# Order of gathers and adds in a routed feed-forward: lists laid out by tile, a third bank for y, weight pieces spread by one line

## The reference

```python
x = x + cross_attention(layernorm(x), ctx)      # 16 x 56 tokens, 1500 context rows of 512 each
h = layernorm(x)                                 # 896 tokens
scores = sigmoid(h @ gate_w.T) + bias            # 16 experts
topk_w, topk_idx = top_k(scores, 4)              # weights normalised to sum 1
out  = sum over the 4 experts e of a token:  w_e * (silu(h @ Wg[e].T) * (h @ Wu[e].T)) @ Wd[e].T
out += silu(h @ Sg.T) * (h @ Su.T) @ Sd.T        # shared expert, all tokens
x = x + out
```

## Time and profile before

| | |
|---|---|
| median of 3 runs | 545.14 us (544.95 to 545.25) |
| profiled execution, its own time | 546.24 us |
| its span | 544.5 us |
| TensorE busy | 481.4 us, 88% |
| VectorE, ScalarE, GpSimd busy | 48%, 29%, 22% |
| issue of a gather on GpSimd, shortest and median | 0.95 and 1.01 us |
| weight loads, issue to landing, median | 7.5 us |
| weight loads start at | 307.97, 315.36, 331.09, 340.44, 348.74, 359.55, 385.94, 407.38, 416.70, 438.94, 455.00 us |

### The profile page before, as it was taken

The page is one execution under the profiler, slowest core; times in us unless marked ns, Lnnn a source line. Parts: engine busy times, 40 slices in busy tenths (PEclk is TensorE's granted clock), DMA queues, the critical chain, the costliest instruction groups (busy, mean ns, idle before and its releaser), DMA issues.

```text
span 544.5 us, 10804 instructions
## 1 busy us (share of the span) xinstructions
PE 481.4 (88%) x2472; PEld 291.5 (54%) x2473; DVE 260.0 (48%) x707; ACT 155.8 (29%) x303; POOL 119.3 (22%) x100
## 2 busy tenths in 40 slices
PE   4999999999999999998789869779998898899960
PEld 1565354453636363543358636567776666676740
DVE  3223345462737354352537864625565466555420
ACT  0001321020202020210213253435455456444430
POOL 1000000000000000000002233335554465335531
PEclk9989999999999999999899979979999899899985
DMA  9999999999999999999646676785858687445452
GB/s 212 393 419 427 398 424 415 409 427 396 424 402 426 403 422 404 422 426 415 258 127 174 150 202 191 235 254 94 221 100 265 137 207 210 78 88 98 98 64 32
DMA packets 28231, 149.04 MB, mean 274 GB/s; under 512 B 4072, under 2 KB 4200, under 8 KB 16424
## 3 DMA queue, kind: packets, MB, share of 16 engines
q1 hardware_dynamic: 15832, 123.08, 57.1%
q0 software_dynamic: 8720, 20.21, 20.5%
q10 hardware_dynamic: 3664, 5.57, 3.3%
HBM read 133.84 MB, written 15.01 MB: 273 GB/s over the span
## 4 chain that ended last, share of the span: by engine, by line
PE 49%; DMA 33%; issue 7%; DVE 3%; ACT 2%; POOLq 1%; ACTq 1%; POOL 1%; DVEq 1%; SPq 0%
DMA ctx_cols<-in_ctx_t 15%; PE b L680 13%; PE scores L550 11%; PE b L574 8%; DMA taken<-h_rows,take_at 8%; DMA out<-y_sb,add_at 5%; PE b L538 4%; PE b L500 4%; PE scores L512 2%; PE scores L680 2%; PE b L564 1%; DMA w_qk<-in_wk 1%; DMA out<-y_sb,shared_at 1%; DMA h_rows<-h 1%; POOL out L459 1%
## 5 line engine op out<-in xcount | busy, mean ns | idle before, releaser
L550 PE MATMUL scores<-ctx_cols,g_t 128*64 128x500 f32 x384 | 85.2, 586 | 2.6 <-DMA ctx_cols<-in_ctx_t 2.5
L574 PE MATMUL b<-ctx_rows,probs_t 125*64 125x512 f32 (+1 forms) x384 | 86.0, 598 | 0.0
L459 POOL DMA_INDIRECT out<-y_sb,add_at x34 | 54.5, 1604 | 89.0 <-ACT add_at L931 46.8
L423 POOL TENSOR_TENSOR rstd<-var_eps,neg_half 128x1 f32<-128x1 f32 x16 | 8.8, 549 | 268.4 <-DVE var_eps L1022 268.4
L680 PE MATMUL b<-w_hi,taken_hi 128*128 x136 | 56.2, 414 | 1.1 <-ACT taken_hi L908 1.1
L680 PE MATMUL b<-w_lo,taken_hi 128*128 x136 | 54.8, 403 | 0.0
L1280 DVE TENSOR_TENSOR w_lo<-w_raw,w_hi (+1 forms) x33 | 39.7, 1223 | 30.2 <-ACT w_hi L897 26.6
L550 PEld LDWEIGHTS scores<-ctx_cols,g_t 128*64 128x64 f32 x384 | 26.1, 136 | 51.8 <-issue 46.0
L574 PEld LDWEIGHTS b<-ctx_rows,probs_t 125*64 125x64 f32 (+1 forms) x384 | 26.3, 137 | 48.0 <-issue 47.1
L444 POOL DMA_INDIRECT taken<-h_rows,take_at x34 | 42.7, 1257 | 28.4 <-DVE take_at L1306 20.2
L897 ACT CAST w_hi<-w_raw (+1 forms) x33 | 33.8, 1047 | 29.0 <-PE b L680 9.1
(11 more groups left out here) (213 smaller groups left out, 677.2 us busy)
## 6 DMA issues: line engine op xcount, KB each, us to landing
ctx_rows<-in_ctx SPq DMA_DIRECT2D x48, 1024.0 KB, 19.5
ctx_cols<-in_ctx_t SPq DMA_DIRECT2D x32, 1500.0 KB, 22.8
w_raw<-in_experts SPq DMA_DIRECT2D x11, 1536.0 KB, 7.5
h_rows<-h ACTq DMA_DIRECT2D x16, 115.5 KB
taken<-h_rows SPq DMA_DIRECT2D x7, 264.0 KB, 3.1
out<-xs ACTq DMA_DIRECT2D x2, 784.0 KB
shared_raw<-in_shared SPq DMA_DIRECT2D x1, 1536.0 KB, 32.4
xs<-in_x ACTq DMA_DIRECT2D x12, 112.0 KB
```

What stands on the lines that cost most here:

```text
L459: nc.gpsimd.indirect_dma_start(out[:, :], bass.IndirectOffsetOnAxis(ap=add_at[i][:, 0:1], axis=0), y_sb[:, i * DIM:(i + 1) * DIM], None, c ...
L550: last = nc.tensor.matmul(scores[HALF * b:HALF * (b + 1), n, 0:CHUNK], g_t[:, k, HALF * b:HALF * (b + 1)], ctx_cols[:, at:at + CHUNK], sta ...
L574: last = nc.tensor.matmul(b3[HALF * b:HALF * (b + 1), :], probs_t[0:rows_in(p), at:at + HALF], ctx_rows[0:rows_in(p), g, b, c * DIM:(c + 1 ...
```

## The change

- **Lists in tile order.** `place_at` holds the 112 columns in float32. TensorE transposes it, ScalarE keeps the transposed copy (`place_t`), and one more matmul with a 0/1 matrix (`tile_picks`) gives 52 columns in the order of the tiles. `tile_rows` makes `tile_at` and `tile_to` from them, so tile t's column is column t-7, without a table. `T_COL` and `T_EXPERT` go; the expert of each tile is a row of `expert_row`, with which `take_weight` now picks the token's weight by comparison over 16 columns. `name_take` waits for these steps.
- **Orders.** VectorE does `take_weight(t+1)` and `name_take(t+3)` before `silu_rows(t)`. A gather waits in addition for the transposes of the tile whose buffer it fills.
- **Three y banks.** y of the expert tiles goes to PSUM banks `(t+1) % 3` of `scores`; ScalarE keeps y(t-3) in the step of tile t. `y_sb` still has two buffers.
- **Scatter columns on GpSimd.** `name_add` goes from ScalarE; `add` copies the column itself, once the add two tiles back has landed. GpSimd's loop is `gather(t+5)`, `add(t)`.
- **Weight pieces.** The count for tile t is (t-6)/34 x 33 + 4, at least what this tile needs (and the next expert's three pieces on the last tile of an expert), at most what the three slots can hold.

```diff
             def gather(t, i):
                 pool.wait_ge(take_named, t - (SHARED - 1))
                 settle(pool)
+                pool.wait_ge(tt_ready, t - 1)
+                settle(pool)
                 nc.gpsimd.indirect_dma_start(
...
             def add(t, i):
                 first = entry(pool, T_FIRST, t - SHARED, TILES + SHARED)
-                pool.wait_ge(added[0], pool.snap((first + 1) // 2 * 16 + 16, min_val=16, max_val=16 * TILES))
+                pool.wait_ge(added[i], t // 2 * 16 + 16)
                 settle(pool)
-                pool.wait_ge(added[1], pool.snap(first // 2 * 16 + 16, min_val=16, max_val=16 * TILES))
-                settle(pool)
-                pool.wait_ge(add_named, t - (SHARED - 2))
+                nc.gpsimd.tensor_copy(add_at[i][:], tile_to[:, bass.ds(t - SHARED, 1)]).then_inc(add_named, 1)
+                others = first // 2 if i == 0 else (first + 1) // 2
+                pool.wait_ge(added[1 - i], pool.snap(others * 16 + 16, min_val=16, max_val=16 * TILES))
                 settle(pool)
                 pool.wait_ge(ysb_ready, t + 1)
+                settle(pool)
+                pool.wait_ge(add_named, t + 1)
...
                     t = pair * 2 + (SHARED + k)
+                    gather(t + 5, k)
                     add(t, 1 - k)
-                    gather(t + 5, k)
...
+            def lay_places():
+                pe.wait_ge(plan_ready, 1)
+                pe.wait_ge(places_ready, 1)
+                nc.tensor.transpose(scores[:, 2, 0:P], place_at[:], ident).then_inc(places_laid, 1)
+            def pick_tiles():
+                pe.wait_ge(places_kept, 1)
+                nc.tensor.matmul(scores[:, 2, P:P + AHEAD], place_t[:], tile_picks[:], start=True, stop=True
+                                 ).then_inc(tiles_picked, 1)
...
             shared_transpose(6)
+            lay_places()
             down(4, 0, shared_hi, shared_lo, 0)
+            pick_tiles()
             up_hi(6, 0, shared_hi, shared_lo, 0)
...
-                keep_y(t - 2, i)
-                if not isinstance(t, int):
-                    name_add(t - 2, i)
+                if not isinstance(t, int) or t > SHARED:
+                    keep_y(t - 3, 1 - i)
                 more_thirds(t + 1)
...
             half(t, 0)
+            keep_y(t - 3, 1)
             keep_y(t - 2, 0)
-            name_add(t - 2, 0)
             keep_y(t - 1, 1)
-            name_add(t - 1, 1)
             z_to_hi(t)
             keep_y(t, 0)
-            name_add(t, 0)
...
+            def tile_rows():
+                dve.wait_ge(tiles_picked, 1)
+                places = scores[:, 2, P:P + AHEAD]
+                ch.mark(nc.vector.tensor_copy(tile_at[:], places))
+                ch.mark(nc.vector.tensor_scalar(wrapped[:], places, float(PAIR_TOKENS), float(TOKENS), ALU.is_lt, ALU.mult))
+                ch.link(nc.vector.tensor_scalar(empty_at[:], places, float(TOKENS), float(PAIR_TOKENS), ALU.is_ge, ALU.mult))
+                ch.link(nc.vector.tensor_tensor(wrapped[:], wrapped[:], empty_at[:], ALU.add))
+                nc.vector.scalar_tensor_tensor(tile_to[:], places, -float(PAIR_TOKENS), wrapped[:], ALU.add, ALU.add
+                                               ).then_inc(tiles_named, 1)
...
             def step(t, i):
                 z_to_lo(t - 1)
+                take_weight(t + 1, 1 - i)
+                name_take(t + 3, 1 - i)
                 silu_rows(t, i)
                 taken_to_lo(t + 1)
-                take_weight(t + 1, 1 - i)
-                name_take(t + 3, 1 - i)
                 more_thirds(t + 1)
```

More of the change, by code:

```diff
@@ L36 @@
 TILES = 48
-TABLES = 8
+TABLES = 6
 SHARED = TOKENS // P
-T_TURNS, T_COL, T_EXPERT, T_PIECES, T_TURN, T_FIRST, T_LOAD, T_HALF = (i * TILES for i in range(TABLES))
+Y_BANKS = 3
+AHEAD = TILES + 4
+T_TURNS, T_PIECES, T_TURN, T_FIRST, T_LOAD, T_HALF = (i * TILES for i in range(TABLES))
 C_ID, C_TRI, C_IOTA, C_REGION = 0, P, 2 * P, 2 * P + EXPERTS
@@ L196, in moe_attention_kernel @@
         fill = sb("fill", [P, LISTS])
[L197 to L200, removed]
+        place_at = sb("place_at", [P, LISTS + EXPERTS])
+        place_t = sb("place_t", [P, P])
+        tile_picks = sb("tile_picks", [P, AHEAD])
+        expert_row = sb("expert_row", [P, AHEAD])
+        picked_w = sb("picked_w", [P, 2 * EXPERTS])
+        wrapped = sb("wrapped", [P, AHEAD])
+        empty_at = sb("empty_at", [P, AHEAD])
+        tile_at = sb("tile_at", [P, AHEAD], i32)
+        tile_to = sb("tile_to", [P, AHEAD], i32)
         behind = sb("behind", [P, 1])
@@ L484, in _ @@
                     t = pair * 2 + (SHARED + k)
+                    gather(t + 5, k)
                     add(t, 1 - k)
-                    gather(t + 5, k)
             t = n_inner * 2 + (SHARED - 2)
-            add(t, 1)
             gather(t + 5, 0)
-            for k in range(1, 6):
+            for k in range(6):
                 add(t + k, 1 - k % 2)
@@ L613, in lay_tables @@
                 last.then_inc(table_rows_ready, 1)
+                for at, column in ((C_PICK, place_col), (C_EXPERT, expert_t)):
+                    last = nc.tensor.matmul(scores[:, 0, at:at + AHEAD], column[:].to_broadcast([P, P]),
+                                            ident[:, 0:AHEAD], start=True, stop=True)
+                last.then_inc(picks_ready, 1)
+            def lay_places():
[6 more added lines that the diff above has]
+                                 ).then_inc(tiles_picked, 1)
             pe.sem_inc(ht_ready, 1)
@@ L709, in down @@
                 settle(pe)
-                if not isinstance(t, int) or t > 1:
+                if not isinstance(t, int):
+                    pe.wait_ge(ysb_ready, t - 2)
+                    settle(pe)
+                elif t > 1:
                     pe.wait_ge(ysb_ready, t - 1)
-                    settle(pe)
+                bank = y_bank(pe, t)
                 for k in range(KI):
-                    part(y_banks[i], zt_hi, hi, at + UP, k, DIM, start=(k == 0))
-                    part(y_banks[i], zt_hi, lo, at + UP, k, DIM)
+                    part(bank, zt_hi, hi, at + UP, k, DIM, start=(k == 0))
+                    part(bank, zt_hi, lo, at + UP, k, DIM)
                 pe.wait_ge(zt_lo_ready, t + 1)
@@ L718, in down @@
                 for k in range(KI):
-                    last = part(y_banks[i], zt_lo, hi, at + UP, k, DIM, stop=(k == KI - 1))
+                    last = part(bank, zt_lo, hi, at + UP, k, DIM, stop=(k == KI - 1))
                 last.then_inc(yt_ready, 1)
@@ L925, in keep_y, with keep_places @@
                 settle(act)
-                nc.scalar.copy(y_sb[:, i * DIM:(i + 1) * DIM], y_banks[i]).then_inc(ysb_ready, 1)
-            def name_add(t, i):
-                col = entry(act, T_COL, t - SHARED, LISTS + EXPERTS - 1)
-                nc.scalar.copy(add_at[i][:], list_to[:, bass.ds(col, 1)]).then_inc(add_named, 1)
+                nc.scalar.copy(y_sb[:, i * DIM:(i + 1) * DIM], y_bank(act, t)).then_inc(ysb_ready, 1)
+            def keep_places():
+                act.wait_ge(places_laid, 1)
+                nc.scalar.copy(place_t[:], scores[:, 2, 0:P]).then_inc(places_kept, 1)
             done = act.alloc_register("act_thirds")
@@ L1154, in _ @@
             nc.vector.tensor_copy(shared_at[:], shared_place[:]).then_inc(shared_named, 1)
-            for rows in (list_at, list_to):
-                ch.mark(nc.vector.tensor_scalar(rows[:, LISTS:], dump_row[:].to_broadcast([P, EXPERTS]), -float(P), None,
-                                                ALU.add))
+            ch.mark(nc.vector.tensor_scalar(place_at[:, LISTS:], dump_row[:].to_broadcast([P, EXPERTS]), -float(P), None,
+                                            ALU.add))
             wide = [P, PAIRS, TILES_MAX]
@@ L1372, in _ @@
             list_rows()
-            dve.wait_ge(plan_ready, 1)
-            name_take(SHARED, 1)
             shared_silu(5)
             taken_to_lo(6)
+            tile_rows()
+            dve.wait_ge(dve_step, ch.now())
+            name_take(SHARED, 1)
             name_take(SHARED + 1, 0)
```

100 lines of the change are left out of this document (59 added, 41 removed).

## The result

The changed kernel takes 554.78 us (551.09 to 556.12, 4 runs) against 545.19 us (544.95 to 548.41, 4 runs) beside it: ratio 1.0155, 95% interval 1.0108 to 1.0202. It is slower; 541.2 was forecast and 548 was the top of the range. Run again it took 553.31 us, ratio 1.0142 (1.0099 to 1.0185).

The account below looks back on a forecast made before the run. The prediction took TensorE's expert-tile transposes, stalled by late gathers, plus the tail as the bound. Hand-over +1.5, start -3.5, pieces -4.7, late gathers -0.7, tail +3.5 gave -3.9 us: 541.2, own range 538.5 to 544, wider 536.5 to 548.

Parts of the forecast that it names:

- The new orders cancel: Steady loop: later y and gather ahead of add leave gathers about where they were, 4.7 instead of 4.98 us; gain 0.7 us.
- No term, but it moves which gathers they hit: Even line: weight loads start one to three tiles sooner and hit other gathers; priced at nothing.
- The third rival: The wait only moves: start gain given back, loads hit first tiles at 2.3 us each; about 545.4 us, chance 0.20.
- The sign that was named: Sign of a wrong forecast: stalls at tiles 23 to 27 of over 5 us together, from loads beside first-tile adds.
- The pieces: Tiles 30 to 32: the even line of weight pieces gains 4.7 us of 6.3 lost, bounds 2.5 and 6.3.
- The start: First expert tiles: gather(12) leaves 4.8 us sooner, add(7) 2.2 later; gain 3.5 us, bounds 1 and 5.5.
- Hand-over: Before tile 7: the new list steps make take_at(7) and its gather 1.5 us later; cost 1.5, bounds 0.5 and 3.
- Tail: After tile 40's transposes: y(37) kept only behind the last tanh, add(37) 4.2 us later; cost 3.5, bounds 2 and 4.5.
- GpSimd's copy: Scatter column copy in GpSimd's add: taken as hidden in the wait for y; bounds nothing to 0.5 us in 29 tiles.
- the slower rival: GpSimd's scatter column copy makes gathers late in most tiles: 552.9 us, or 547 at half the tiles; chance 0.20.

Follow-up runs that it names:

- 5: The changed kernel run again, nothing altered: 553.31 us, ratio 1.0142 to the kernel before.
- 7: The changed kernel with y kept one tile earlier, at t-2 as before: 541.32 us, ratio 0.9909.
- 3: The changed kernel loading only 64 of 3072 weight columns for experts past the third (stale weights): 536.93 us, ratio 0.9755.
- 4: The kernel before, loading only 64 of 3072 weight columns for experts past the third (stale weights): 536.00 us, ratio 0.9734.
- 9: The changed kernel with the scatter column copied by ScalarE instead of GpSimd: 548.32 us, ratio 1.0065.
- 1: The changed kernel with the old table of weight pieces: 552.17 us, ratio 1.0072.
- 18: The changed kernel with the old table of weight pieces, run again in a later group: 550.50 us, ratio 1.0083.
- 17: The changed kernel with the old table of weight pieces and the scatter column copied by ScalarE: 550.61 us, ratio 1.0095.
- experiment 2: The kernel before with only the new even line of weight pieces added: 548.40 us, ratio 1.0031.
- 8: The changed kernel with y kept at t-2 and zt_hi of tile 40 ahead of y of tile 39: 540.14 us, ratio 0.9906.
- 16: The changed kernel with y at t-2, tile 40's zt_hi ahead of tile 39's y, old piece table; a repeat: 537.55 us, ratio 0.9779.
- 10: The changed kernel with y at t-2, tile 40's zt_hi ahead of tile 39's y, old piece table: 536.83 us, ratio 0.9840.
- 14: The changed kernel with the scatter column copied by ScalarE and small weight loads past the third expert: 535.48 us, ratio 0.9744.
- 15: The changed kernel with y at t-2, tile 40's zt_hi first, old piece table, scatter column copied by ScalarE: 537.32 us, ratio 0.9773.

## Why the prediction was wrong

**The new orders cancel: right, but a gain was given away.** The forecast said that y one tile later and the gather ahead of the add leave each gather at the same place, 4.7 us behind the tile that frees its buffer. It leaves at 4.65 where nothing is late. But the forecast took the late y as given and never priced it: against y kept at t-2 it costs 12.0 us (5 and 7), by the two spans 4.8 of it in the tail and 6.9 between T(7) and T(40), where the gathers have less room.

**"No term, but it moves which gathers they hit": the step that failed.** The forecast gave nothing for loads that fall on other gathers and adds. Measured: +7.2 us in T(16) to T(30), +6.7 when run again, and -2.3 without the traffic (3 against 4), so it is the traffic that costs. With 1.2 us of margin, a load beside the add ahead of a first tile and the next load beside the gather behind it cost 6 us at a time, and the changed kernel has that twice. The third rival had the mechanism at 2.3 us for each, but its sum holds only 0.7 us for it, and its 545.4 is 9 us short. The sign that was named, stalls at tiles 23 to 27, did not come (tile 23 waited 1.2 us); the stalls are at tiles 17 to 19, 28 and 29.

**Is it the even line, with its sooner loads? That stays open.** T(16) to T(30) is 79.60 us before. In kernels with the late y and full loads it is, with the line, 86.77, 86.27 and, with the copy on ScalarE (9), 78.41; with the old table 84.90 (1), 80.93 (18) and 80.13 (17). In 18 a load starts at 386.44, within 0.5 us of where it was before, and tile 18 still waits 3.9 us for a gather issued at 385.25. So the same orders with any of these places of the loads give anything from no loss to 7 us. By the ratios two pairs say that the line costs 0.6 to 0.8% (1.0155 and 1.0142 with it, 1.0072 and 1.0083 without), and with y early 0.9906 stands against 0.9840 and 0.9779. The pair with the copy on ScalarE says the opposite (9 with the line 1.0065, 17 without it 1.0095), and in the kernel before experiment 2 leaves it open (0.9977 to 1.0085). No group has both tables with full loads on one set of orders, and of these pairs only 8 and 16 have intervals that do not meet. With the old table the changed kernel is still 0.7 to 0.8% slower; in the profiles of 1 and 18 T(7) is 2.4 and 1.4 us later, T(16) to T(30) 5.3 and 1.3 longer, T(32) to T(40) 0.8 and 0.7, and the tail 3.8, less what the start and the pieces gave.

**The pieces: right size, half the cause.** Forecast -4.7 for T(30) to T(32), measured -4.6 and -4.7. But the line alone gives -2.5 (2), and the changed kernel with the old table already has 12.56 (1) and 13.76 (18) for 16.59. VectorE's triple steps before and in experiment 1, each time ScalarE's three pieces, VectorE's three, and TensorE behind them:

```profile
463.20 2.95 ACT L897 CAST w_hi<-w_raw  x3 [2.16 <-PE b L680]
...
466.19 3.50 DVE L1280 TENSOR_TENSOR w_lo<-w_raw,w_hi  x3 [1.76 <-ACT w_hi L897]
...
470.16 1.19 PE L680 MATMUL scores<-w_hi,zt_lo 128*128 x2 [2.02 <-DVE zt_lo L1315]
```
```profile
467.44 2.95 ACT L948 CAST w_hi<-w_raw  x3 [1.05 <-PE scores L725]
...
468.82 3.56 DVE L1337 TENSOR_TENSOR w_lo<-w_raw,w_hi  x3 [1.59 <-ACT w_hi L948]
...
472.87 0.70 PE L725 MATMUL scores<-w_hi,zt_lo 128*128 x2 [0.32 <-DVE zt_lo L1375]
```

VectorE starts 2.99 us behind ScalarE before, and 1.38 in experiment 1: the same three pieces end early enough. With y early and full loads the line did not help there at all (15.08 us in kernel 8, against 13.96 and 13.84 with the old table in 10 and 16). Which of the new orders moved VectorE was not tried.

**The start: half of it.** Forecast -3.5, measured -1.8. The step was right: gather(12) leaves at 345.75 and not 348.47, tile 12's wait of 5.21 us is gone, and smaller ones stand at tiles 13 (1.46) and 14 (2.45).

```profile
345.75 0.98 POOL L466 DMA_INDIRECT taken<-h_rows,take_at  x1 [0.30 <-issue]
346.74 0.66 POOL L475 COPY add_at<-tile_to 128x1 int32 x1
351.93 1.61 POOL L483 DMA_INDIRECT out<-y_sb,add_at  x1 [4.54 <-issue]
```

T(10) to T(14) falls from 28.96 to 27.14, 1.8 us. add(7), at 351.93, is 6.1 us later than before, where 2.2 was forecast: y(6) is kept from 342.4 and not 340.87, add(6) goes at 343.87, and beside the load of 342.68 it takes 6.96 us to land where the forecast had 5.5. The gather of tile 13 stands behind it. That took the other half, as far as the rows show.

**Hand-over: the sum right, its steps not. Tail: right.** T(7) is 1.9 later against 1.5, and tile 7 waits 4.88 us. VectorE's first and last step of the hand-over:

```profile
312.81 0.21 DVE L1264 CAST tile_at<-scores 128x52 int32<-128x52 f32 x1 [0.69 <-PE scores L652]
...
313.67 0.20 DVE L1358 COPY take_at<-tile_at 128x1 int32<-128x1 int32 x2
```

take_at(7) is there at 313.67, 0.5 us behind the earlier trace rows and not 1.5; the gather leaves at 314.81 and its rows are used 8.1 us later, where before it was 6.8. With small loads, which leave the first three experts' loads as they are, T(7) is 2.6 us late. What lengthens that landing stays open. The tail is +4.1 against +3.5, by the step that was named.

**GpSimd's copy: the slower rival's price is refuted, but the copy is not always hidden.**

```profile
L475 POOL COPY add_at<-tile_to x34: 181/199/1038, 346.7 to 539.3; 128x1 int32 x34
```

A median of 0.199 us (the forecast's nearest row was 0.55), 1.04 at most, and mostly in the time in which the add waits for y; experiments 14, 15 and 17 find no cost in every tile. Where y is already there the add waits for the copy: four adds did, 3.4 us in all, add(13) at 389.18 among them, and the gathers of tiles 19 and 29 left 0.8 to 0.9 us later than without it (experiment 9). The forecast took the copy as hidden everywhere. (It also called 1.01 us the least issue of a gather; that is the median, and the least is 0.95.) That the time landed beyond this rival's 547 to 553 is not by its mechanism in the main.

**T(32) to T(40), +1.3, was in no term.** It is there with small loads too (43.33 against 42.18). Tiles 29, 30 and 31 are each the first of an expert; the gathers of tiles 36 and 37 leave 6.94 and 8.02 us behind T(t-2), where before those of 33, 35 and 36 were the late ones, of which 33 hid under the triple pieces. Why this costs 1.3 us was not taken further.

## What to carry to other kernels

Where indirect transfers are issued in order by one engine, work out how much room each has before its reader stalls, and then let every bulk load fall beside it once. In this kernel the margin was 1 us and a landing went from 4.5 to 8 or 9 us beside a load, so a plan that shifts either the loads or the transfers needs a term for it, with a range as wide as the loss. Removing the traffic and keeping every instruction is a cheap test that separates what the traffic costs from what the orders cost. An operation that is hidden while its engine waits for something else comes back onto the path where that wait is short: look at the cases in which the chain is already late, not at the median. When a deeper buffer lets a step move later, ask what stands behind that step, since here keeping y as early as before beside the new third bank was worth 12 us, more than the rest of the change together.

## What the runs showed of the hardware

- **An indirect transfer of 128 rows beside a 1.5 MB load.** In the chains of the kernel before, of the changed one and of its second run, behind 350 us: 4.0 to 5.0 us with no load moving (three times 5.2 to 5.9), 5.4 to 8.8 us with a load started between 3.7 us ahead of the transfer and 1.6 us behind its issue. In kernel 7 an accumulating one issued 1.3 to 2.0 us ahead of a load took 9.3 to 9.9 us. The Trainium skill, DMA: Bandwidth & Descriptors, Latency and other measured facts, says that a transfer's fixed cost is smaller under a lighter load on HBM, whose access takes 0.2 us on average and 2 us at high load. The direction agrees; the growth here, up to 4 or 5 us, is larger than that. Whether HBM or the queues of the 16 engines make it was not tried.
- **GpSimd's 128x1 copy** takes 0.2 us at the median but 0.66 to 1.04 in single cases, and 0.76 to 0.77 in the four of the tail that start 1.0 us behind an indirect issue of 1.57 to 1.60 us and overlap it. Between a gather and an add that is ready it lengthens the distance from 1.28 to 2.04 us (9 against the changed kernel).
- **Scatter between executions.** The kernel before took from 540.0 to 557.8 us over this study's runs. Kernels with small loads keep within 3.5 us over four to six runs, but kernels 10, 15 and 16, with full loads, y early and the old table, keep within 4.2 us over six, so the loads alone do not make it. The 95% intervals of the ratios reach 0.2 to 0.9% to either side.
